# A conditioning MLP over 16 batches: other orders of the work around h, and the DMAs of the turned h issued by ScalarE

## What is computed

```
h = _ln(x, pw_g[pathway_ids], pw_b[pathway_ids])
h = _ln(h, cp_g[compartment_ids], cp_b[compartment_ids])
t = _ln(x, tm_g[time_steps], tm_b[time_steps])
m, n, r = x + _mlp_ln(memory / noise / resource state)     # one row per batch
s = _ln(x, ms_g[scale_type], ms_b[scale_type])
cat = concatenate([w[0]*h, w[1]*t, w[2]*m, w[3]*n, w[4]*r, w[5]*s])
out = x + _mlp_ln(cat)      # silu(cat @ int_W1 + b1) @ int_W2 + b2, then a layer norm
```

## Time and profile before

| | |
|---|---|
| time, median of 3 runs | 998.59 us (990.33 to 999.7) |
| time of the profiled execution | 992.41 us |
| its span, first to last instruction | 990.7 us |
| TensorE busy | 956.3 us, 97% |
| VectorE busy | 802.9 us, 81% |
| ScalarE busy | 271.4 us, 27% |
| GpSimd busy | 455.5 us, 46% |

### The profile page before, as it was taken

How to read it: one execution, slowest core, us unless ns; L and a number is a source line. 1 busy time by engine, 2 the same in 40 slices (tenths; PEclk the granted TensorE clock), 3 DMA queues, 4 the chain that set the end, 5 groups by cost and what they waited for, 6 DMA issues and landing times. The chain is left out here.

```text
span 990.7 us, 13506 instructions
## 1 busy us (share of the span) xinstructions
PE 956.3 (97%) x4196; PEld 773.7 (78%) x4196; DVE 802.9 (81%) x1183; ACT 271.4 (27%) x341; POOL 455.5 (46%) x619
## 2 busy tenths in 40 slices
PE   7999998999999999999999999999999999999997
PEld 6677877778877787887888888777877878787885
DVE  6887969788696878979787896978869697896965
ACT  4532232231322213223231322223132222313211
POOL 3335244445443554445455444545544355454322
PEclk9999999999999999999999999999999999999999
DMA  9956363847548465563847456384664838466362
GB/s 312 324 215 192 103 196 117 244 105 238 149 141 228 137 209 131 174 198 119 262 139 225 125 184 187 119 249 126 217 146 145 238 117 242 97 211 171 96 149 64
DMA packets 97425, 174.33 MB, mean 176 GB/s; under 512 B 10216, under 2 KB 48872, under 8 KB 93440
## 3 DMA queue, kind: packets, MB, share of 16 engines
q1 hardware_dynamic: 74432, 108.04, 33.8%
q0 software_dynamic: 22976, 66.07, 25.0%
HBM read 141.33 MB, written 32.75 MB: 176 GB/s over the span
## 5 line engine op out<-in xcount | busy, mean ns | idle before, releaser
L1440 PE MATMUL hid_ps<-cat_hi,w_hi 128*128 128x512 f32 x1008 | 394.1, 391 | 7.5 <-DVE cat_lo L961 7.1
L1441 PE MATMUL hid_ps<-cat_lo,w_hi 128*128 128x512 f32 x1008 | 392.5, 389 | 0.0
L1442 PE MATMUL hid_ps<-cat_hi,w_lo 128*128 128x512 f32 x1008 | 392.4, 389 | 0.0
L1440 PEld LDWEIGHTS hid_ps<-cat_hi,w_hi 128*128 128x128 f32 x1008 | 189.2, 188 | 53.3 <-DVE cat_lo L961 11.3
L1442 PEld LDWEIGHTS hid_ps<-cat_hi,w_lo 128*128 128x128 f32 x1008 | 189.2, 188 | 39.7
L1441 PEld LDWEIGHTS hid_ps<-cat_lo,w_hi 128*128 128x128 f32 x1008 | 189.3, 188 | 38.9
L555 POOL DMA_INDIRECT pw_rows<-cp,class_now x64 | 103.0, 1610 | 162.5 <-DVE y_sb L969 152.3
L734 ACT ACTIVATE cat_hi<-v_ring 128x1024 fp32r<-128x1024 f32 x64 | 67.9, 1062 | 335.5 <-DVE v_ring L951 335.4
L548 POOL DMA_INDIRECT pw_rows<-pw,path_now x64 | 75.5, 1179 | 83.6 <-DVE y_sb L994 71.4
L569 POOL DMA_DIRECT2D r_sb<-x x60 | 57.6, 959 | 108.0 <-DVE r_sb L1056 99.6
L1537 PE MATMUL o_ps<-w_hi,hid_hi 128*128 128x512 f32 x240 | 93.4, 389 | 0.0
(11 more groups left out here) (170 smaller groups left out, 1209.2 us busy)
## 6 DMA issues: line engine op xcount, KB each, us to landing
x_sb<-xp SPq DMA_DIRECT2D x16, 1024.0 KB, 4.8
out<-r_sb SPq DMA_DIRECT2D x64, 256.0 KB, 4.0
xc<-xT SPq DMA_DIRECT2D x15, 1024.0 KB, 10.2
h_turned<-y_sb SPq DMA_DIRECT2D x60, 256.0 KB, 6.4
r_sb<-x POOLq DMA_DIRECT2D x60, 256.0 KB, 5.4
v_ring<-h_turned SPq DMA_DIRECT2D x60, 256.0 KB, 4.1
stats_bc<-token_stats SPq DMA_DIRECT2D x30, 256.0 KB, 5.5
ids_sb<-ids SPq DMA_DIRECT2D x16, 256.0 KB, 5.8
```

The source lines that it names most:

```text
L1440: pe.matmul(acc, w1_hi[:, k, cols], hi, start=start, stop=False)
L1441: pe.matmul(acc, w1_hi[:, k, cols], lo, start=False, stop=False)
L1442: return pe.matmul(acc, w1_lo[:, k, cols], hi, start=False, stop=stop)
```

## The change

Four things change.

1. ScalarE issues `h_write`, between `ts_high(b,2)` and `ts_high(b,3)`; SP no longer does. SP issues `h_read(b,0)` ahead of `load_xT(b+1)` and `h_read(b,1)` behind it.
2. All four `y_mul` of batch b+1 stand in DVE's batch b, ahead of `h_low(b,1)`, and wait for `h_out` (the write has landed) instead of `h_lo_done`. The first two `y_add` of b+1 stay at the end of batch b; no `y_norm` stands there any more. The turns of b stand around and right behind `ts_mult(b,2)`. `centre(b+1)` comes ahead of the last `out_sum`, both `x_low` ahead of the last `out_stats`.
3. GpSimd does `out_rstd(b-1,0)` ahead of the four gathers, and gathers all class rows of b+1 in batch b.
4. Batch 1 has the order of the others on DVE, ACT and PE, and the prologue is reordered to fit: batch 1's `x_stats` come sooner on DVE, four gathers ahead of `x_rstd(1)` on GpSimd, `fill(1,0)` ahead of `first_pair(1)` on TensorE.

The core of the diff:

```diff
@@ SP, chunk
-                if not by_pe(b):
-                    h_write(b)
+                if not first:
+                    h_read(b, 0)
                 if not (first or last):
                     load_xT(b + 1)
-                if not by_pe(b):
-                    h_read(b, 0)
+                if not first:
                     h_read(b, 1)
@@ ACT
+            def h_write(b):
+                act.wait_ge(y_turned, TT * b)
+                for g in range(P // 32):
+                    act.dma_start(h_dram[:, :, g * P:(g + 1) * P].rearrange("a r c -> r a c"),
+                                 y_sb[32 * g:32 * g + 32, :, :].rearrange("r f (a c) -> r (f a) c", c=P)).then_inc(h_out, 16)
...
+                ts_high(b, 1)
+                for t in range(TT):
+                    y_hat(b, t)
+                ts_high(b, 2)
+                h_write(b)
+                ts_high(b, 3)
                 h_high(b, 0)
+                h_high(b, 1)
@@ DVE, y_mul
-                wait(dve, h_lo_done, 2 * b)
+                if isinstance(b, int) and b == 1:
+                    dve.wait_ge(filled, FT + 2)
+                elif not (isinstance(b, int) and b == 0):
+                    dve.wait_ge(h_out, 64 * (b - 1))
@@ DVE, the new chunk from the second out_sum on
+                out_sum(b - 1, 1)
+                h_low(b, 0)
+                out_stats(b - 1, 2, o_ps[:, 0, :])
+                if not last:
                     turn_stats(b + 1)
+                out_sum(b - 1, 2)
+                if not last:
+                    for t in range(TT):
+                        y_mul(b + 1, t)
+                h_low(b, 1)
@@ PE, first_chunk and chunk: batch 1 now like the others
+                fill(b, 0)
+                first_pair(b)
+                fill(b, 1)
+                pair(b, 1)
+                second(b - 1, 0)
```

More of the change, by code:

```diff
@@ L1213, in first_chunk @@
                     y_norm(0, t)
-                w_low(13)
+                for t in range(TT):
+                    x_stats(1, t)
                 nets_stats()
                 h_low(0, 0)
+                w_low(13)
                 w_low(14)
                 w_low(15)
[L1219 to L1226, removed]
@@ L1227, in first_chunk @@
                 pack_first()
                 turn_stats(1)
+                h_low(0, 1)
+                class_rows()
+                nets_norm()
+                x_low(1, 0)
                 x_low(1, 1)
+                nets_weigh()
+                y_mul(1, 0)
+                y_mul(1, 1)
                 onehot_next(1)
-                for t in range(TT):
-                    y_mul(1, t)
+                centre(1)
+                scaled_next(1)
+                y_mul(1, 2)
+                y_mul(1, 3)
@@ L1233, in first_chunk, with chunk @@
                 y_add(1, 0)
                 add_b1()
-                scaled_next(1)
-                centre(1)
-                for t in range(1, TT):
-                    y_add(1, t)
-            def chunk(b, last=False):
-                if isinstance(b, int) and b == 1:
-                    ts_mult(b, 0)
-                    hidden_low(b - 1, 0)
-                    ts_low(b, 0)
-                    hidden_low(b - 1, 1)
+                y_add(1, 1)
+            def chunk(b, first=False, last=False):
+                ts_mult(b, 0)
+                hidden_low(b - 1, 0)
+                ts_low(b, 0)
+                hidden_low(b - 1, 1)
+                if first:
@@ L1259, in chunk @@
+                y_norm(b, 0)
+                y_norm(b, 1)
+                ts_low(b, 1)
+                y_norm(b, 2)
+                y_norm(b, 3)
+                y_turn(b, 0)
+                ts_mult(b, 2)
+                y_turn(b, 1)
+                y_turn(b, 2)
+                y_turn(b, 3)
+                ts_low(b, 2)
+                if first:
                     dve.wait_ge(rows_bc_in, 16)
-                    out_stats(b - 1, 0, o_ps[:, 0, :])
-                    ts_mult(b, 3)
+                out_stats(b - 1, 0, o_ps[:, 0, :])
@@ L1262, in chunk @@
+                if not last:
                     x_stats(b + 1, 0)
                     x_stats(b + 1, 1)
-                    ts_low(b, 3)
-                    out_stats(b - 1, 1, o_ps[:, 1, :])
-                    out_sum(b - 1, 0)
+                out_sum(b - 1, 0)
+                ts_mult(b, 3)
+                if not last:
                     x_stats(b + 1, 2)
                     x_stats(b + 1, 3)
-                    out_sum(b - 1, 1)
-                    out_stats(b - 1, 2, o_ps[:, 0, :])
@@ new lines, in chunk @@
+                ts_low(b, 3)
+                out_stats(b - 1, 1, o_ps[:, 1, :])
+                out_sum(b - 1, 1)
+                h_low(b, 0)
+                out_stats(b - 1, 2, o_ps[:, 0, :])
+                if not last:
+                    turn_stats(b + 1)
+                out_sum(b - 1, 2)
+                if not last:
+                    for t in range(TT):
+                        y_mul(b + 1, t)
+                h_low(b, 1)
+                if not last:
+                    x_low(b + 1, 0)
+                    x_low(b + 1, 1)
```

139 lines of the change are left out of this document (24 added, 115 removed).

## The result

The changed kernel takes **963.7 us** (median of 4 runs, 962.55 to 964.26), the kernel before 994.46 in the same comparison (986.27 to 999.7): ratio 0.970, interval 0.962 to 0.978. The execution whose trace follows took 963.4 us, with a span of 961.7 against 990.7, so 29.0 us of span are won. The sign of the forecast was right and its size too small: 22.0 us were forecast.

A forecast was written before the change was run, and what follows sets the result against it. TensorE, busy 97%, was taken as the floor, its idle time coming from a loop of late h and waiting DVE. 21.7 + 1.7 - 1.0 - 0.4 = 22.0 us off 992.4 gave 970.4 us, range 966 to 976 (eight in ten: 965 to 984).

The forecast's parts named there:

- the third `ts_mult` at T+16.2: DVE's batch, T being the start of `fill(b,0)`: third `ts_mult` starts at T+16.2, once `fill(b,2)` is done.
- the write at T+19.3: After the third `ts_mult` and three turns, the write of h is issued at T+19.3, before at T+28.7.
- `h_low(b,1)` done at T+46.6 at worst: DVE ahead of `last_pairs`: done 0.8 us before TensorE needs it at T+47.4, counting 17.1 us from write to `h_high`.
- About 9 us: Body: time from the turn of the statistics to `scaled`, putting `scaled` near T+52 with hardly a wait.
- One batch with hardly a wait took 57.34: TensorE's body: 57.34 us taken as a batch's pace, giving 21.7 us of excess over 13 batches.
- a loss of 1.0: Prologue and batch 1: first pair waits for a later `add_b1`, net 1.0 us lost, bounds -0.8 and +6.
- 1.7 won in batch 1: Batch 1 took 59.07 us on TensorE, so it carries 1.7 us more excess to win.
- The bound of +6 for late statistics: Prologue: upper bound of the loss, +6 us, if batch 1's statistics come as late as before.
- 17.1 was taken: Issue of the write to `h_high`: 17.1 us, measured before, used as bound; 14.0 from medians was the other.
- rival "slower": `h_low(b,1)`: `h_out` or gathered rows 5 us late make TensorE idle about 4 us a batch, 1026 us; chance 0.04.
- That removes the 12.3 us group even if h were no earlier: `fill`: bringing `ts_mult(b,0)` 2.0 us forward to T+5.6 alone removes TensorE's 12.3 us wait for `ts_mult`.
- rival "only the 12.3 goes": Body: the loop was not the cause, h is as late as before, 979 us; chance 0.10.

The follow-up runs named there:

- n4: Changed kernel with batch 1's token statistics late in the prologue, where they stood in the kernel before; 971.88 us, ratio 0.978.
- p1: m1 with GpSimd holding its four gathers until the write of h has landed; 1031.07 us, ratio 1.039.
- m1: Changed kernel with h's four turns back behind `ts_mult(b,2)`, `ts_low` and `out_stats`, as they stood before; 1047.09 us, ratio 1.055.
- p4: Changed kernel with the four gathers ahead of `out_rstd(b-1,0)` on GpSimd, so the first starts ahead of the write; 963.51 us, ratio 0.972.
- o1: Changed kernel with the DMA part undone: SP issues the write, then the x load, then both reads; all other orders as changed; 1006.8 us, ratio 1.020.
- n2: Changed kernel with SP issuing the x load ahead of both reads of h, the write still on ScalarE; 1003.13 us, ratio 1.013.
- n1: Changed kernel with SP instead of ScalarE issuing the four writes of h, right ahead of the first read; 963.59 us, ratio 0.969.
- b1: Kernel before with only the DMA part: ScalarE issues the writes, SP the first read ahead of the x load; 1037.03 us, ratio 1.050.
- b2: Kernel before with only SP's order changed: first read ahead of the x load, the write still on SP; 1039.37 us, ratio 1.054.
- p6: m1 with DVE's four `y_mul(b+1)` behind `h_low(b,1)` instead of ahead of it; 1025.08 us, ratio 1.034.
- m3: Changed kernel with 8 spare statistics operations (4.8 us) put ahead of `h_low(b,1)` on DVE; 978.35 us, ratio 0.985.

## Why the prediction was right or wrong

**Right: TensorE's waits in the body go, and with them its loss.** The forecast had the third `ts_mult` at T+16.2 (measured 16.2 to 17.9), the write at T+19.3 (19.2 to 20.9), `h_low(b,1)` done at T+46.6 at worst (43.1 to 44.8), and no waiting of TensorE in the body. That was the mechanism, and it is what happened. Two steps on the way were off without moving the time. "About 9 us" from the turn of the statistics to `scaled` was 14.3 in batch 8, so `scaled` waits, where the forecast had "hardly a wait". The first `ts_mult`, by the forecast within T+3, comes up to T+4.2; `fill(b,1)` at T+6.8 still finds it done.

**Wrong in size: the pace, 2.9 us.** "One batch with hardly a wait took 57.34" was taken as the floor. The floor is 57.12. In that batch of before two starts of PE come 0.11 and 0.06 us later than the pace, most of the 0.22 and too short for the view of waits: 13 x 0.22 = 2.9 us more to be won. With this term right the forecast is 967.5, and a range set as wide around it, 963.1 to 973.1, holds the 963.7.

**Wrong in size: the prologue, 3.0 us.** It was put at a loss of 1.0, set against 1.7 won in batch 1; 3.7 was won. The rows that answer to the earlier trace rows:

```profile
67.83 0.21 DVE L873 STREAM_TRANSPOSE pack_rows<-pack_cols 128x32 f32<-128x32 f32 x1
...
76.64 2.29 DVE L885 TENSOR_TENSOR xc<-xc,stats_bc 128x2048 f32<-128x2048 f32 x1
78.85 0.75 DVE L920 SCALAR_TENSOR_TENSOR scaled<-ids_sb,small_sb,stats_bc 128x512 fp32r<-128x512 int32 x1
...
83.03 0.66 DVE L1132 TENSOR_SCALAR batch_bias<-o_ps,small_sb 128x16 f32<-128x16 f32 x4 [0.42 <-PE o_ps L1356]
```

The turn was at 67.8, not 70; the statistics were there 8.8 us after it, not 11.9; `add_b1` was at 83.0, not 87.5. The 11.9 was read rightly, but most of it was the time of two DMAs, which were quicker after. SP's rows, before and then after, and the landing of the reads before:

```profile
77.58 0.33 SPq L393 DMA_DIRECT2D token_stats<-pack_rows  x1
82.56 1.29 SPq L399 DMA_DIRECT2D stats_bc<-token_stats  x2
DMA to landing us min/median/max: 5.1/5.5/5.9
```
```profile
68.08 0.33 SPq L385 DMA_DIRECT2D token_stats<-pack_rows  x1
71.35 1.29 SPq L391 DMA_DIRECT2D stats_bc<-token_stats  x2
```

The write took 5.0 us before and 3.3 after; the last read had landed 6.6 us after 82.56 before (at 89.1, just ahead of `scaled` at 89.19), and at most 5.3 after 71.35 now. Why they were faster no run shows. TensorE passes from batch 0 to batch 1 without a gap. The bound of +6 for late statistics was right: by it prologue and batch 1 give 1.7 - 6 = -4.3, and n4 shows 3.7 - 8.2 = -4.5. The other 0.7 us, of the last batch, were not counted, and 0.4 was kept back for restarts that don't occur: 2.9 + 3.0 + 0.7 + 0.4 = 7.0, and 22.0 + 7.0 = 29.0.

**Wrong, though it moved no number: how the write goes.** From write to split, 17.1 was taken and 14.0 was the other bound; it is 13.6. Against the rival "slower" stood that "the gathers met the write before as well", and by that 17.1 should have stayed. The new order takes the write *out* of the gathers' way. In every traced kernel in which the gathers start ahead of it or with it, the landing takes 11.4 to 12.9 us on average, and where they start later 6.5 to 7.8; p1 shows it as cause, for against m1 only the gathers are moved. But p4 shows that this isn't what makes the changed kernel fast.

**Wrong: that the small moves suffice.** "That removes the 12.3 us group even if h were no earlier" holds to the letter (the group is gone in o1) and not for the time, since the wait returns at `h_low`: o1 is slower than before. The rival "only the 12.3 goes", 979 us, had no mechanism behind it. And the x load's place on SP got one sentence and no price; it is worth 39 us (n2 against after). Of the single moves tried on after only the turns are worth more, 83 us (m1).

**Right: the issuing engine is worth nothing.** n1 against after, 963.6 to 963.7, and b1 against b2, 1037 to 1039. The Trainium skill's page DMA: Bandwidth & Descriptors, "Issuing engines are not separate DMA queues", says that issuing from several engines saves only the time of the issuing, and the runs agree.

**Why it takes both halves.** The new orders begin `y_mul` in the batch ahead and turn earlier: A falls from 21.2 to 17.2 and C from 16 to 13, but the four `y_mul` come into B. With the x load ahead of the reads B is 29.8 and eats it all; with the first read ahead, 24.0. With the old orders the same SP order makes B 25.3 against 21.4, with A and C about as they were. What `y_mul` in the batch ahead is worth by itself no run shows: it was moved back only together with the late turns (p6), where that gained 22 us.

## What to carry to other kernels

When an in-order engine waits for a DMA chain that it starts itself, cut its round trip at that chain and add the pieces over one batch. While the sum lies below the other engine's pace a delay costs nothing (m3 took in 4.0 us, p4 a late write); above the pace every piece counts, and work that only goes from one piece to another gains little (p6). Price the place of each large load in its queue as carefully as the instructions, with the loads and gathers of other queues that will be in flight then. Take the floor from the distance of back-to-back starts, not from the best batch of a kernel that waits.

## What the runs showed of the hardware

- A long wait of TensorE costs more than its length. After the wait of 4.07 us in m1 the granted clock was at the lower level, 1.2 GHz, for some 5 us, and 12 matmuls took 2.4 us more. In m3's trace, with ten waits of at most 1.6 us, it stayed at the upper level from 30 to 960 us.
- 1 MB written by four DMAs alone in flight went at 157 GB/s over the 6.7 us (p1); beside four gathers and a read of 256 KB the same write took 13.4 us, while all DMAs together moved 254 GB/s (m1). In the DMA view of the two stretches (300.8:314.2 and 298.4:305.1), the write's queue (packets, MB, share of the 16 engines), m1 first:

```profile
q10 hardware_dynamic: 2112, 1.05, 34.5%
```
```profile
q10 hardware_dynamic: 2112, 1.05, 68.2%
```
